# Two convolution layers on one core: the second layer's short chains, its residual and its statistics rearranged

## What is computed

```python
x = x + _L0_conv_ref(_gn(x), ...)   # deformable attention: offsets and weights by a 3x3 convolution,
                                    # bilinear samples of v at 9 taps, weighted sum, 1x1 projection Wo
x = x + _L1_conv_ref(_gn(x), ...)

def _L1_conv_ref(x, ...):
    p1 = relu(conv3x3(x, p1_w) + p1_b);  pool1 = top_pool(p1)    # running maximum from below
    p2 = relu(conv3x3(x, p2_w) + p2_b);  pool2 = left_pool(p2)   # running maximum from the right
    p_gn1 = group_norm(conv3x3(pool1 + pool2, p_w), p_gn_g, p_gn_b)
    gn1 = group_norm(conv1x1(x, c1_w), gn1_g, gn1_b)
    return relu(conv3x3(relu(p_gn1 + gn1), c2_w) + c2_b)
```

## Time and profile before

| | us |
|---|---|
| median of 3 runs | 156.76 |
| lowest and highest | 155.72, 157.32 |
| the profiled execution | 156.15 |
| its span | 154.3 |
| PE busy | 131.8 (85%) |
| DVE busy | 111.5 (72%) |
| ACT busy | 59.0 (38%) |

### The profile page before, as it was taken

One profiled execution on the slowest core, in us unless ns is written; L12 is line 12 of the kernel. 1 busy time (PEld: TensorE's weight loads), 2 busy tenths in 40 slices (PEclk: granted clock), 3 DMA queues, 4 the chain that ended last, 5 costly groups with the idle time before them and its releaser, 6 DMA issues.

```text
span 154.3 us, 3278 instructions
## 1 busy us (share of the span) xinstructions
PE 131.8 (85%) x1399; PEld 112.3 (73%) x1399; DVE 111.5 (72%) x197; ACT 59.0 (38%) x107; POOL 18.5 (12%) x27
## 2 busy tenths in 40 slices
PE   4976499998997999999999989998599996676780
PEld 3754499997997999998998968876376564334460
DVE  5518993395399996999969999983681878766702
ACT  3009449839905591076812180110010607003311
POOL 8931120000000000000080000000011010110100
PEclk9999879999999999999999999999999999999999
DMA  4970000049652000000000000000000000000014
GB/s 117 236 131 0 0 0 4 0 147 259 145 130 57 2 4 0 0 4 0 0 0 0 4 0 0 0 4 2 2 0 4 6 4 0 4 0 0 0 38 102
DMA packets 6675, 5.43 MB, mean 35 GB/s; under 512 B 4657, under 2 KB 5939, under 8 KB 6659
## 3 DMA queue, kind: packets, MB, share of 16 engines
q1 hardware_dynamic: 5986, 4.19, 11.8%
q10 hardware_dynamic: 672, 1.02, 2.8%
HBM read 2.79 MB, written 0.52 MB: 21 GB/s over the span
## 4 chain that ended last, share of the span: by engine, by line
PE 49%; DVE 25%; issue 8%; ACT 6%; DMA 6%; POOL 1%; SPq 1%; POOLq 0%; DVEq 0%
PE bank L980 10%; PE bank L999 9%; PE bank L1024 8%; PE bank L972 7%; DVE prod L742 6%; DMA prod<-in_w_off 6%; PE bank L933 4%; DVE part L769 3%; DVE x_t L868 3%; PE bank L1122 3%; PE bank L1155 3%; PE bank L949 2%; DVE wy L777 2%; DVE pooled L874 2%; DVE bn L594 1%
## 5 line engine op out<-in xcount | busy, mean ns | idle before, releaser
L742 DVE TENSOR_TENSOR prod<-hat,wy 128x1440 f32<-128x1440 f32 (+3 forms) x25 | 27.3, 1161 | 0.0
L769 DVE TENSOR_TENSOR part<-v,bank 128x1280 f32<-128x1280 f32 (+3 forms) x20 | 21.5, 1111 | 7.8 <-PE bank L1024 4.3
L933 PE MATMUL bank<-ones_r 128*128 128x512 f32 x83 | 23.2, 436 | 2.1 <-POOL w_pair L371 2.1
L999 PE MATMUL bank<-cst,prod 128*128 128x128 f32 (+3 forms) x189 | 22.3, 272 | 0.8 <-DVE prod L742 0.8
L999 PEld LDWEIGHTS bank<-cst,prod 128*128 128x128 f32 (+3 forms) x189 | 20.7, 132 | 1.4 <-DVE prod L742 1.0
L1024 PE MATMUL bank<-cst,part 128*128 128x128 f32 x168 | 20.9, 274 | 0.8 <-DVE part L769 0.3
L933 PEld LDWEIGHTS bank<-ones_r 128*128 128x128 f32 x83 | 17.0, 212 | 5.8 <-POOL w_pair L371 2.1
L1024 PEld LDWEIGHTS bank<-cst,part 128*128 128x128 f32 x168 | 18.3, 140 | 2.0 <-DVE part L769 1.7
L980 PE MATMUL bank<-w_cross,g_cross 128*128 128x216 f32 x144 | 19.5, 283 | 0.0
L980 PEld LDWEIGHTS bank<-w_cross,g_cross 128*128 128x128 f32 x144 | 18.2, 200 | 0.0
L972 PE MATMUL bank<-w_pair,g_pair 128*128 128x216 f32 x96 | 14.8, 294 | 3.5 <-ACT g_cross L431 3.5
(11 more groups left out here) (93 smaller groups left out, 151.6 us busy)
## 6 DMA issues: line engine op xcount, KB each, us to landing
v<-v SPq DMA_DIRECT2D x2, 480.0 KB, 6.0
v<-v SPq DMA_DIRECT2D x2, 448.0 KB, 5.6
prod<-in_w_off ACTq DMA_DIRECT2D x1, 486.0 KB, 7.1
prod<-in_w_off SPq DMA_DIRECT2D x1, 486.0 KB, 8.8
w_s<-in_w SPq DMA_DIRECT2D x4, 72.0 KB, 3.7
wc_s<-in_wc SPq DMA_DIRECT2D x2, 144.0 KB, 3.3
wp_s<-in_wp SPq DMA_DIRECT2D x4, 72.0 KB, 2.5
x_b<-in_x SPq DMA_DIRECT2D x1, 256.0 KB, 4.6
```

What stands on the lines that cost most here:

```text
L742: return nc.vector.tensor_tensor(prod[:, 0:K2 * CELLS * cx].rearrange("p (k q s) -> p q k s", k=K2, s=cx)[:, q0:q0 + nd], hat[:, c % 2, d0 ...
L769: nc.vector.tensor_tensor(part[:, n % PARTS, 0:nd, 0:cv].rearrange("p d (q e) -> p d q e", e=HD), moved, weights.unsqueeze(3).to_broadcast ...
L933: nc.tensor.matmul(ps.rearrange("p (a q) -> p a q", q=P), ones_r[:, :], ones_r[:, :].unsqueeze(1).to_broadcast([P, 4, P]), start=True, sto ...
L999: last = nc.tensor.matmul(out_ps[0:size, b * P:(b + 1) * P], prod[:, at:at + size], ident, start=(b == 0 and t == 0), stop=(b == n - 1 and ...
```

## The change

1. The residual is added by chunks: a pair of adds (one per column parity) for all four images of the columns of chunk c-1 stands in chunk c, ahead of the fourth apply. Only the last chunk's pair stands behind the last `y0`. `x1` moves to memory of its own for this.
2. The far code on DVE becomes one loop over all rows with one loop over all columns in it (13 steps beside two memsets).
3. In the second layer's statistics the square and add (L599, L600) fall away. PE makes a second matmul against a new matrix `C_GD`, half the signed difference of the two channel means, and `pair_variance` adds its square to the averaged variance. The constants' second load grows by 128 columns, 64 KB.
4. The first input of the second layer is written by DVE alone, (x1 - mean) * rstd, both images; no `affine`, nothing on ACT. Both pairs' group means stand ahead of the first convolution, with `WARM_IN = (5, 4, 0)`.
5. The order on DVE and ACT changes: `pools(1)` before `c1_stats(1)`, `branches(1)` before `affine_c(0)`; the means of C1 and P of the first group move into `pool_conv(1)`.
6. At the end DVE makes max(conv, -c2_b) + (x1 + c2_b) in one instruction; ACT has made x1 + c2_b earlier. SP stores both halves of the even steps, ACT those of the odd ones.

```diff
-WARM_IN = (11, 14)
+WARM_IN = (5, 4, 0)
...
+    c[:, C_GD:C_GD + P] = c[:, C_GB:C_GB + P] * np.where(i[:, None] == i[None, :], 1, -1)
...
-        res = u_flat[:, 0:HALF * HW].rearrange("p (n q) -> p n q", q=HW)
+        res, x1_b = (u_flat[:, i * HALF * HW:(i + 1) * HALF * HW].rearrange("p (n q) -> p n q", q=HW)
+                     for i in range(2))
...
-            return bank[b][:, q:q + 2 * DUO]
+            return bank[b][:, q:q + 3 * DUO]
...
-            for n in range(HALF):
+            for n in range(0, HALF, 2):
                 sp.wait_ge(res_ready, n + 1)
-                sp.dma_start(out_d[n], res[lo, n, :]).then_inc(stored, 16)
+                for half, rows in enumerate((lo, hi)):
+                    sp.dma_start(out_d[n, half], res[rows, n, :]).then_inc(stored, 16)
             sp.wait_ge(stored, 2 * 16 * HALF)
...
-            act.wait_ge(borders, 1)
-            for g in range(2):
-                n = DUO * g
-                act.wait_ge(norm_ready, G_IN + g + 1)
-                nc.scalar.activation(inner(g1, n, 1)[:, 0], rows_cols(x1[:, n, :]), ACT.Identity,
-                                     bias=ab[:, G_IN + g, 3, 0:1],
-                                     scale=ab[:, G_IN + g, 2, 0:1]).then_inc(g1_ready, 1)
...
+            act.wait_ge(x1_ready, 1)
+            nc.scalar.activation(x1_b, x1[:, :, :], ACT.Identity, bias=vec_s[:, 4:5]).then_inc(x1_b_ready, 1)
             branches(0)
+            branches(1)
             affine_c(0)
-            branches(1)
+            affine_c(1)
             second_input(0)
-            affine_c(1)
             second_input(1)
-            outputs(0)
-            outputs(1)
-            for n in range(HALF):
+            for n in range(1, HALF, 2):
                 act.wait_ge(res_ready, n + 1)
-                act.dma_start(out_d[HALF + n], res[hi, n, :]).then_inc(stored, 16)
+                for half, rows in enumerate((lo, hi)):
+                    act.dma_start(out_d[n, half], res[rows, n, :]).then_inc(stored, 16)
...
-                link(last)
-                link(nc.vector.tensor_tensor(sq[:, s, 0:cols], mv[:, s, 0:cols, 0], mv[:, s, 0:cols, 0], ALU.mult))
-                nc.vector.tensor_tensor(mv[:, s, 0:cols, 1], mv[:, s, 0:cols, 1], sq[:, s, 0:cols],
-                                        ALU.add).then_inc(stats_in, 1)
+                if s == G0:
+                    link(last)
+                    link(nc.vector.tensor_tensor(sq[:, s, 0:cols], mv[:, s, 0:cols, 0], mv[:, s, 0:cols, 0], ALU.mult))
+                    last = nc.vector.tensor_tensor(mv[:, s, 0:cols, 1], mv[:, s, 0:cols, 1], sq[:, s, 0:cols], ALU.add)
+                last.then_inc(stats_in, 1)
...
+            def pair_variance(s):
+
+                ve.wait_ge(stats_ps, s + 1)
+                means, apart = pair_stats(s)[:, 0:2 * DUO].rearrange("p (n t) -> p t n", t=2), pair_stats(s)[:, 2 * DUO:]
+                link(nc.vector.tensor_copy(sq[:, s, 0:DUO], apart))
+                link(nc.vector.tensor_tensor(sq[:, s, 0:DUO], apart, sq[:, s, 0:DUO], ALU.mult))
+                nc.vector.scalar_tensor_tensor(ab[:, s, 1, 0:DUO], means[:, 1], EPS, sq[:, s, 0:DUO],
+                                               ALU.add, ALU.add).then_inc(var_ready, 1)
+                link(nc.vector.tensor_copy(ab[:, s, 0, 0:DUO], means[:, 0]))
 
...
-                for r0, r1, ranges in FAR_ROWS:
-                    per_row = 5 + sum(i1 - i0 for i0, i1 in ranges) * CELL
-                    with ve.Fori(r0, r1) as k:
-                        base = n + (k - r0) * per_row
-                        ve.wait_ge(far_v, (k + 1) * 16)
-                        base = run(base, row_steps(k))
-                        for i0, i1 in ranges:
-                            base = columns(base, i0, i1)
-                        ve.sem_inc(far_row_done, 1)
-                    n += per_row * (r1 - r0)
+                with ve.Fori(0, FULL) as k:
+                    ve.wait_ge(far_v, (k + 1) * 16)
+                    base = run(first + k * per_row, row_steps(k))
+                    with ve.Fori(0, FULL) as i:
+                        run(base + i * CELL, cell_steps(i))
+                    ve.sem_inc(far_row_done, 1)
...
+            def add_input(par, j0, j1):
+
+                def columns(t):
+                    return t[:, :, :].rearrange("p n (y j a) -> p a j y n", a=2, j=W // 2)[:, par, j0:j1]
+                return nc.vector.tensor_tensor(columns(x1), y0_banks[par][:, :].rearrange(
+                    "p (j y n) -> p j y n", y=H, n=HALF)[:, j0:j1], columns(x_b), ALU.add)
+
+            def residual(c):
+
+                x0, w = CHUNKS[c]
+                ve.wait_ge(y0_ps, c + 1)
+                for par in range(2):
+                    last = add_input(par, x0 // 2, (x0 + w) // 2)
+                return last
...
-                for i in APPLY[:-1]:
+                for m, i in enumerate(APPLY[:-1]):
+                    if c and m == ND - 2:
+                        residual(c - 1)
                     apply(i)
...
+            residual(NC - 1).then_inc(x1_ready, 1)
+
+            def x1_stats(g):
                 norm_stats(G_IN + g, [x1[:, DUO * g + j, :] for j in range(DUO)])
 
             def first_input(g):
-                n = DUO * g + 1
-                ve.wait_ge(norm_ready, G_IN + g + 1)
-                nc.vector.tensor_scalar(inner(g1, n, 1)[:, 0], rows_cols(x1[:, n, :]), ab[:, G_IN + g, 2, 1:2],
-                                        ab[:, G_IN + g, 3, 1:2], ALU.mult, ALU.add).then_inc(g1_half, 1)
-
-            x1_stats(0, residual(0))
-            variance(G_IN, DUO, pair_stats(G_IN))
-            added = residual(1)
-            affine(G_IN, DUO)
+                s = G_IN + g
+                ve.wait_ge(rstd_ready, s + 1)
+                for j in range(DUO):
+                    n = DUO * g + j
+                    nc.vector.tensor_scalar(inner(g1, n, 1)[:, 0], rows_cols(x1[:, n, :]), ab[:, s, 0, j:j + 1],
+                                            ab[:, s, 2, j:j + 1], ALU.subtract, ALU.mult).then_inc(g1_ready, 1)
+
+            ve.wait_ge(x1_ready, 1)
+            x1_stats(0)
+            pair_variance(G_IN)
+            x1_stats(1)
             ve.wait_ge(borders, 1)
             first_input(0)
-            x1_stats(1, added)
-            variance(G_IN + 1, DUO, pair_stats(G_IN + 1))
-            affine(G_IN + 1, DUO)
+            pair_variance(G_IN + 1)
             first_input(1)
+            ve.wait_ge(ld_vec, 32)
+            nc.vector.tensor_scalar(neg_b[:, :], vec_s[:, 4:5], -1.0, None, ALU.mult).then_inc(neg_ready, 1)
...
+            def results(g):
+                ve.wait_ge(o_ps, g + 1)
+                for k in range(DUO):
+                    n = DUO * g + k
+                    nc.vector.scalar_tensor_tensor(res[:, n, :], pair_banks(OUT_BANK[g])[:, k], neg_b[:, 0:1],
+                                                   x1_b[:, n, :], ALU.max, ALU.add).then_inc(res_ready, 1)
+
             c1_stats(0)
             pools(0)
-            c1_norm(0)
+            pair_variance(G_C1)
+            c1_affine(0)
+            pools(1)
             c1_stats(1)
-            pools(1)
-            c1_norm(1)
             p_stats(0)
+            pair_variance(G_C1 + 1)
+            pair_variance(G_P)
+            c1_affine(1)
             both_branches(0)
             p_stats(1)
+            pair_variance(G_P + 1)
             both_branches(1)
-            for n in range(HALF):
-                ve.wait_ge(relu_ready, n + 1)
-                nc.vector.tensor_tensor(res[:, n, :], res[:, n, :], x1[:, n, :], ALU.add).then_inc(res_ready, 1)
+            ve.wait_ge(neg_ready, 1)
+            ve.wait_ge(x1_b_ready, 1)
+            results(0)
+            results(1)
...
+            def group_mean(s):
+
+                pe.wait_ge(stats_in, s + 1)
+                stat = pair_stats(s)
+                nc.tensor.matmul(stat[:, 0:2 * DUO], cst[:, C_GB:C_GB + P],
+                                 mv[:, s, 0:DUO, :].rearrange("p n t -> p (n t)"), start=True, stop=True)
+                nc.tensor.matmul(stat[:, 2 * DUO:], cst[:, C_GD:C_GD + P], mv[:, s, 0:DUO, 0], start=True,
+                                 stop=True).then_inc(stats_ps, 1)
...
             keep_warm(WARM_IN[0], bank[0][:, :])
-            group_means(G_IN, DUO, pair_stats(G_IN), (C_GB,))
+            group_mean(G_IN)
             keep_warm(WARM_IN[1], bank[0][:, :])
-
-            def group_mean(s):
-                group_means(s, DUO, pair_stats(s), (C_GB,))
+            group_mean(G_IN + 1)
+            keep_warm(WARM_IN[2], bank[0][:, :])
...
-                pe.wait_ge(g1_ready, g + 1)
-                pe.wait_ge(g1_half, g + 1)
-                branch_conv(g, {6: G_IN + 1} if g == 0 else {4: G_C1})
+                pe.wait_ge(g1_ready, DUO * (g + 1))
+                branch_conv(g, {4: G_C1} if g else {})
                 skip_conv(g)
-            pool_conv(0, {4: G_C1 + 1})
-            pool_conv(1, {6: G_P})
```

(58 more changed lines are left out.)

28 lines of the change are left out of this document (2 added, 26 removed).

## The result

The changed kernel took 152.0 us in the median of four runs (151.03 to 153.74), the kernel before 156.94. The ratio is 0.969, with an interval of 0.961 to 0.977. The medians are of all runs, the ratios leave out runs more than 1.5% above the fastest of their version. Forecast were 151.4 us and a range of 149.6 to 153.4. The profiled execution took 151.03 us with a span of 149.2, against 156.15 and 154.3.

The account below looks back on a forecast made before the run. It took an alternating PE and DVE chain as the bound, with a branch hole, dummies and second-layer waits for DVE. Gains of 4.6 + 0.3 = 4.9 us off 156.15 gave 151.2, as a median 151.4; range 149.6 to 153.4.

Parts of the forecast that it names:

- The pairs in the chunks: Residual adds in chunks 3 and 4 lie on the path, 0.6 us each, 1.2 us later; chunks 1 and 2 cost nothing.
- The hole: DVE's idle on "issue" at the far_displacements branch, before the last residual; the shorter far body ends it, gaining 1.81 us.
- Up to the first convolution: From the last y0 at 108.36 through residual, statistics and input writing; first convolution at 113.3 instead of 115.34.
- The branches and the new order: Second layer, first branch convolution to pool_conv(1): with pools(1) earlier on DVE, pool_conv(1) starts at 128.7 against 133.12.
- The end: From pool_conv(1) at 128.7 to out_conv(1) at 141.2 against 145.80, finishing at 145.3; then the output stores.
- the tail: After PE's last matmul: fused DVE instructions and two ACT issues take 2.17 instead of 2.52 us, gain 0.35.
- The clock rival: Between last y0 and first convolution, too few dummies let the clock fall, costing at most 1.7 us: 153.1; chance 0.07.
- the argument that pauses below 0.9 us are safe: Between last y0 and first convolution, PE's longest pause is about 0.9 us; offered against a clock fall.
- rival 1: At DVE's far branch the stall stays, the target still out of reach; everything behind moves by 1.8 us: 153.2; chance 0.15.
- the two parts named for it: Range's lower end: pairs at 0.4 each and smaller waits than summed (0.8), with the scatter of runs (0.8).

Follow-up runs that it names:

- the two versions whose first pause is filled: Changed kernel with 33 instead of 18 dummies in the first layer's start, alone (ratio 0.960) or with two pairs of adds moved behind the flag (0.958).
- both edits: Changed kernel with the adds of chunks 2 and 3 moved behind the flag and 33 instead of 18 first-layer start dummies: 149.87 us median, ratio 0.958.

## Why the prediction was right

The direction, the size and the chain were as forecast; 4.9 us were summed and 5.03 measured between the profiled executions. By its own steps:

- **The pairs in the chunks.** Taken 1.2 us, measured 0.59 + 0.56 = 1.15. The scaling by elements from L828 held, and chunks 1 and 2 cost nothing: wy of chunks 2 and 3 are 18.10 us apart after, 18.11 before.
- **The hole.** Taken 1.81, measured 1.81 when removed from the kernel before. Shown is that the hole goes and comes with the long body, in both kernels. That it is a fetch is inferred, and the packet of the earlier trace rows was weak evidence for it, since the changed kernel has such a packet without a hole. The rule that the Trainium skill states in "Runtime: NRT & Kernel Launch", instruction fetch mechanics, agrees with the hole's coming and going. How much code may lie between was not tried.
- **Up to the first convolution.** From y0's end 4.94 us forecast, 4.70 measured: the two images take 0.71 in place of 0.84, since the second starts before the first has ended. The mean of the second pair was taken as hidden with 0.2 to spare. It ended at 113.63 and the images at 112.89 + 0.71 = 113.60, so it is hidden with nothing to spare.
- **The branches and the new order.** 15.4 us forecast from the first convolution to pool_conv(1), 15.01 measured. Along the chain of work the scans and adds took 3.46 and 3.5 in place of 3.6, as a scan starts shortly before the instruction ahead of it has ended. The order alone is worth 2.5 us by its experiment.
- **The end.** 12.5 and 12.42 us; the tail 0.35 and 0.39.
- **What the sum left out.** The first 79 us came out 0.73 later, with the clock at 0.50 for 6.8 us instead of 3.4. I had set everything ahead of chunk 3 to zero. The sizes of the other terms erred by 0.8 us the other way, so it is luck that the total fits better than its parts. The version with the old end had the short stretch (18.2 to 21.6) and reached wy of chunk 3 at 79.11, as the kernel before did at 79.17. So it is the clock, and no part of the change, that moved this stretch.
- **The clock rival.** Neither trace of the changed kernel shows it between the layers. But three of eight traces with its nine dummies do, 3.4 us long, and it cost 1.5 and 1.7 us in the two where it lay under the branch convolution (6.16 and 6.33 us from the first to the second, instead of 4.65). So the price of such a stretch was right. The chance of 0.07 looks too low, though eight traces of six versions and the changed kernel don't give a rate: in the two versions whose first pause is filled, five of ten executions had a mean clock of 0.997 or more and so none of these stretches. The step that failed is the argument that pauses below 0.9 us are safe. With longer pauses the stretch lasted 6.8 us, in three versions, twice the length that the price assumed, and without dummies it cost 2.5 us in the trace. I had also treated the rivals as apart. With the hole present the few dummies don't hold the clock: rival 1 would have cost 3.5 us, not 1.8, and put the time at about 155, outside the range. (The range's lower end lies 1.8 us below the forecast, while the two parts named for it give 1.6.) The short far code and the small number of dummies depend on each other.

## What to carry to other kernels

Count waits in the order of time: by the trace half of this gain was an order in which no engine does less work; what the others wait for is only done first. A branch that is never taken isn't free when the code that it jumps over is long; the sign is an idle of 3.3 to 3.5 us on "issue" behind the branch, which went when the body was cut from 89 steps to 13. An instruction packet in that place says nothing alone, since the kernel without the hole has one too. A pause on PE has two prices, itself and the clock behind it, so an edit that shortens dummies has to be tried together with what else lengthens the pause.

## What the runs showed of the hardware

- The same program starts chunk 3 at 79.9 or 80.3 us by where stretches of 3.4 or 6.8 us at the granted clock of 0.50 fall in its first layer. The latest case seen among all versions was 81.60 (the version with the old number of dummies between the layers, at 0.50 for 3.4 us from 9.3 and for 6.8 from 19.5), and the earliest 78.95 (both edits, no such stretch). This is larger than several terms of the sum.
- Pauses of PE of 1.6 to 2.0 us between short matmuls, with five dummies or none in front, were followed by 6.8 us at 0.50 in three versions. A pause of 1.79 us behind the eleven dummies of the earlier trace rows, in the kernel before, was not the earlier trace rows. With nine dummies and pauses of 0.25 and 0.73 us both outcomes occurred, 1.00 throughout or 3.4 us at 0.50, in programs that issue nearly the same matmuls there. What decides between them stays open.
- Adds in this access pattern cost, for two: 0.45 us with 64 elements each, 0.67 with 128, 1.15 with 256, 2.22 with 512. That is 0.9 to 1.1 us per 256 more elements each, which leaves about 0.2 for the pair as a fixed part (an estimate from these four rows).
